# First attention: key sums by column quarters, and sums by feature computed with the head's sums as the stationary operand

## The reference

```python
logits = jnp.einsum('bhld,hdf->bhlf', k, W0) - 0.5 * jnp.sum(k * k, axis=-1, keepdims=True)
alpha = jax.nn.softmax(logits.reshape(B, H, L * NF), axis=2).reshape(B, H, L, NF)
N = jnp.einsum('bhlf,bhld->bhfd', alpha, v)      # key sums
D = jnp.sum(alpha, axis=2)
phi = jax.nn.softmax(jnp.einsum('bhld,hdf->bhlf', q, W0), axis=-1)
num = jnp.einsum('bhlf,bhfd->bhld', phi, N)
den = jnp.einsum('bhlf,bhf->bhl', phi, D)
out = num / (den[..., None] + EPS)
```

## Time and profile before

| | |
|---|---|
| median of three runs | 936.79 us |
| profiled execution, its own time | 937.28 us |
| its span, first to last instruction | 934.3 us |
| TensorE busy | 897.4 us, 96% |
| weight loads | 668.3 us, 72% |
| VectorE busy | 628.6 us, 67% |
| ScalarE busy | 307.8 us, 34% |
| GpSimd busy | 316.2 us, 34% |
| mean granted TensorE clock | 0.996 |

### The profile page before, as it was taken

The page is one execution under the profiler, slowest core; times in us unless marked ns, Lnnn a source line. Parts: engine busy times, 40 slices in busy tenths (PEclk is TensorE's granted clock), DMA queues, the critical chain, the costliest instruction groups (busy, mean ns, idle before and its releaser), DMA issues.

```text
span 934.3 us, 15873 instructions
## 1 busy us (share of the span) xinstructions
PE 897.4 (96%) x6316; PEld 668.3 (72%) x6316; DVE 628.6 (67%) x940; ACT 307.8 (33%) x494; POOL 316.2 (34%) x309
## 2 busy tenths in 40 slices
PE   6989999999999999999999998999999999999998
PEld 3668778877745444889976785888776445449998
DVE  4767566467554657978868574765774555778887
ACT  3645555210154445201133355641002443450000
POOL 5212412222375778356610023210005544771000
PEclk9999999999999999999999999999999999999999
DMA  8104000433143643366530000012222010216562
GB/s 272 38 22 136 1 1 1 142 99 112 60 136 88 210 135 76 104 176 187 159 118 1 2 1 1 2 53 90 67 81 79 1 26 2 68 37 179 177 198 91
DMA packets 46719, 80.07 MB, mean 86 GB/s; under 512 B 13047, under 2 KB 24023, under 8 KB 46647
## 3 DMA queue, kind: packets, MB, share of 16 engines
q1 hardware_dynamic: 46647, 79.07, 27.9%
HBM read 59.55 MB, written 19.33 MB: 84 GB/s over the span
## 4 chain that ended last, share of the span: by engine, by line
PE 83%; DVE 8%; issue 3%; ACT 2%; DMA 2%; POOL 1%; SPq 0%; POOLq 0%; DVEq 0%; ACTq 0%
PE ps L1213 19%; PE ps L1587 10%; PE ps L1492 6%; PE ps L1520 5%; PE ps L1432 5%; PE ps L1593 5%; PE ps L1386 5%; PE ps L1221 5%; PE ps L1338 3%; PE ps L1456 3%; PE ps L1400 3%; PE ps L1353 3%; DVE region L1057 2%; PE ps L1255 2%; PE ps L1292 2%
## 5 line engine op out<-in xcount | busy, mean ns | idle before, releaser
L611 POOL TENSOR_TENSOR xT<-xT,region 128x1024 f32<-128x1024 f32 (+5 forms) x80 | 127.7, 1596 | 92.2 <-PE ps L1520 63.8
L1132 DVE COPY_PREDICATED region<-region,ps 128x512 f32<-128x512 uint32 x112 | 82.5, 736 | 66.5 <-PE ps L1213 65.9
L1587 PE MATMUL ps<-expert_hi,k_hi 128*128 128x256 f32 x512 | 126.1, 284 | 0.7 <-DVE k_hi L1116 0.6
L1587 PE MATMUL ps<-expert_lo,k_hi 128*128 128x256 f32 x512 | 124.7, 281 | 0.0
L1057 DVE TENSOR_REDUCE region<-ps 128x2 f32<-128x1024 f32 (+2 forms) x96 | 89.0, 956 | 46.6 <-PE ps L1466 27.7
L1213 PE MATMUL ps<-expert_hi,wide_hi 128*128 128x512 f32 x256 | 102.3, 400 | 0.0
L1213 PE MATMUL ps<-expert_hi,wide_lo 128*128 128x512 f32 x256 | 99.9, 390 | 0.0
L1213 PE MATMUL ps<-expert_lo,wide_hi 128*128 128x512 f32 x256 | 99.8, 390 | 0.0
L1587 PEld LDWEIGHTS ps<-expert_hi,k_hi 128*128 128x128 f32 x512 | 97.3, 190 | 3.4 <-issue 3.4
L1587 PEld LDWEIGHTS ps<-expert_lo,k_hi 128*128 128x128 f32 x512 | 97.4, 190 | 0.0
L1116 DVE TENSOR_TENSOR k_hi<-region 128x1024 fp32r<-128x1024 f32 x64 | 80.7, 1262 | 19.9 <-PE ps L1593 19.7
(11 more groups left out here) (157 smaller groups left out, 1718.9 us busy)
## 6 DMA issues: line engine op xcount, KB each, us to landing
region<-hot_rows SPq DMA_DIRECT2D x128, 128.0 KB, 3.3
expert_hi<-halves_kept SPq DMA_DIRECT2D x22, 384.0 KB, 3.5
expert_lo<-halves_kept SPq DMA_DIRECT2D x22, 384.0 KB, 4.2
halves_kept<-expert_hi SPq DMA_DIRECT2D x16, 512.0 KB, 5.4
halves_kept<-expert_lo SPq DMA_DIRECT2D x16, 512.0 KB, 6.2
expert<-in_value_experts SPq DMA_DIRECT2D x8, 512.0 KB, 4.5
expert<-in_output_experts SPq DMA_DIRECT2D x8, 512.0 KB, 4.5
gb<-scale_rows SPq DMA_DIRECT2D x16, 256.0 KB, 3.9
```

The source lines that it names most:

```text
L611: pool.tensor_tensor(acc(c)[:, heads, lo:CH], acc(c)[:, heads, lo:CH], PT[:, k % RING, heads, lo:CH], ALU.add).then_inc(sem["added"], 1)
L1132: dve.copy_predicated(V3[:, t].rearrange("p (h k) -> p h k", k=HD3), chosen.unsqueeze(2).broadcast_to([P, H3, HD3]), ps[:, n % 4, :].rearr ...
L1587: mm(ps[:, 4 + t // 2, t % 2 * D:(t % 2 + 1) * D], k_hi[n % 2][:, t * P:(t + 1) * P], w[:, slot, columns], start=(n == 0 and t % 2 == 0 an ...
```

## The change

The key sums use four 32-column quarters of the array: one head at a time, 32 stationary columns (17 of them its own), 64 moving columns, 128 products for 64. N1w becomes 8 blocks of 32 columns, one copy instead of six, with no clearing; one epsilon product and one addition instead of three.

num is computed the other way round: `sums_turned(t)` takes a head's sums as the stationary operand (64 rows by 32 columns) and the turned features (64 rows by 128 columns) as the moving one, 16 products into banks 4 and 5. ScalarE copies the result (numT, 128x512), and 4 transposes bring it into bank 6. `sums_turned` stands right behind f in a step.

The first attention's maxima and subtractions are one instruction each of 1024 elements. In both attentions the product with Wo (now bank 7) and its VectorE work come ahead of num and its quotient, the norm's transposes use bank 5, and ScalarE copies the turned rows (`norm_evac`) ahead of the next `norm_apply`.

```diff
-    HALF = P // 2
+    HALF, QUARTER = P // 2, P // 4
 
     H1, HD1, NF = 16, 16, 64
     V1W = HD1 + 1
     PAIRS1 = H1 // 2
-    WIN = 3 * 2 * V1W
+
+    PAIR_AT = [4 * (k // 2 % 2) + 2 * (k // 4) + k % 2 for k in range(PAIRS1)]
...
-        V1_all = view((TT - 1) * H1 * V1W + (PAIRS1 - 1) * 2 * V1W + WIN)
+        V1_all = view(TT * H1 * V1W + HALF - 2 * V1W)
...
-        N1w = view(PAIRS1 * WIN).rearrange("p (k w) -> p k w", k=PAIRS1)
+        N1w = view(H1 * QUARTER // 2).rearrange("p (k w) -> p k w", k=PAIRS1)
+        N1_dens = N1w[:, :, HD1]
         at[0] = 0
-        N1T = view(CH)
+        N1T = view(2 * P)
+        numT = view(CH)
...
-        N1_RUNS = [(0, 1, 0), (1, PAIRS1 - 1, 2 * V1W), (PAIRS1 - 1, PAIRS1, 4 * V1W)]
...
-            return 7 if a else 3 if b else 4 + t % 2
+            return 5 if a else 3 if b else 4 + t % 2
...
-                until(pool, "oT_ready", b, 0)
-                pool.memset(N1w, 0.0).then_inc(sem["windows_clear"], 1)
-                until(pool, "windows_clear", b, 1)
...
-                        copy(N1T, ps[:, 4, :], "n_sb")
+                        copy(N1T, ps[:, 4, 0:2 * P], "n_sb")
+                    if 0 <= (t := s - 2) < TT:
+                        until(act, "numT_ps", b, t + 1)
+                        if t:
+                            until(act, "num_ps", b, t)
+                        copy(numT.rearrange("p (i s) -> p i s", i=2), ps[:, 4:6, 0:2 * P], "numT_sb")
...
+                    for a, t in due(s, 6):
+                        norm_evac(b, a + 1, t)
                     for a, t in due(s, 5):
                         norm_apply(b, a + 1, t)
                     for a, t in due(s, 6):
-                        norm_evac(b, a + 1, t)
...
                 def place_sums():
 
                     until(dve, "nT_ps", b, 1)
-                    until(dve, "windows_clear", b, 1)
-                    nT = ps[:, 5, :].rearrange("p (k w) -> p k w", w=HALF)
-                    for k0, k1, w0 in N1_RUNS:
-                        dve.tensor_copy(N1w[0:HALF, k0:k1, w0:w0 + V1W], nT[0:HALF, k0:k1, 0:V1W]
-                                        ).then_inc(sem["n_blk"], 1)
-                        dve.tensor_copy(N1w[HALF:P, k0:k1, w0 + V1W:w0 + 2 * V1W], nT[HALF:P, k0:k1, V1W:2 * V1W]
-                                        ).then_inc(sem["n_blk"], 1)
+                    dve.tensor_copy(N1w.rearrange("p k w -> p (k w)"), ps[:, 5, 0:2 * P]).then_inc(sem["n_blk"], 1)
 
...
+                        if a == 0:
+                            f = ps[:, 2:4, :].rearrange("p g (h f) -> p (g h) f", f=F)
+                            o = phi[:, i, 0:H * F].rearrange("p (h f) -> p h f", f=F)
+                            m = top[:, i, 0:H]
+                            dve.tensor_reduce(m, f, AX.X, ALU.max).then_inc(sem["top_ready"], DA)
+                            if s == 2:
+                                place_sums()
+                            if t >= 2:
+                                until(dve, "fT_ps", b, t - 1)
+                            until(dve, "top_ready", b, (t + 1) * DA)
+                            dve.tensor_tensor(o, f, m.unsqueeze(2).broadcast_to([P, H, F]), ALU.subtract
+                                              ).then_inc(sem["f_sub"], 1)
+                            continue
...
                         until(dve, "za_ps", b, 1)
-                        for k0, k1, w0 in N1_RUNS:
-                            dens = N1w[:, k0:k1, w0 + HD1:w0 + 2 * V1W:V1W]
-                            dve.tensor_tensor(dens, dens, ps[:, 6, 2 * k0:2 * k1].rearrange("p (a i) -> p a i", i=2),
-                                              ALU.add).then_inc(sem["n_ready"], 1)
+                        dve.tensor_tensor(N1_dens, N1_dens, ps[:, 6, 0:PAIRS1], ALU.add
+                                          ).then_inc(sem["n_ready"], 1)
+                    for a, t in due(s, 4):
+
+                        until(dve, "y_ps", b, a * TT + t + 1)
+                        until(dve, "bias_added", b, a * TT + t + 1)
+                        step(dve.tensor_tensor(X[:, b, t, :], ps[:, 7, 0:D], X[:, b, t, :], ALU.add))
+                        norm_stats(b, a + 1, t)
...
+                        until(dve, "num_ps", b, a * TT + t + 1)
+                        if a == 0:
+                            pairs = ps[:, 6, :].rearrange("p (i k w) -> p k i w", i=2, w=QUARTER)
+                            scale = rc[:, i, 0:H].rearrange("p (k i) -> p k i", i=2)
+                            step(dve.reciprocal(scale, pairs[:, :, :, HD]))
+                            if t >= 2:
+                                until(dve, "cxT_ps", b, t - 1)
+                            dve.tensor_tensor(cx[:, i, :].rearrange("p (k i w) -> p k i w", i=2, w=HD),
+                                              pairs[:, :, :, 0:HD],
+                                              scale.unsqueeze(3).broadcast_to([P, PAIRS1, 2, HD]),
+                                              ALU.mult).then_inc(sem["cx_ready"], 1)
+                            continue
                         num = ps[:, 6, 0:H * W].rearrange("p (h w) -> p h w", w=W)
...
-                    for a, t in due(s, 4):
-
-                        until(dve, "y_ps", b, a * TT + t + 1)
-                        until(dve, "bias_added", b, a * TT + t + 1)
-                        step(dve.tensor_tensor(X[:, b, t, :], ps[:, 5, 0:D], X[:, b, t, :], ALU.add))
-                        norm_stats(b, a + 1, t)
...
+                def sums_turned(t):
+
+                    until(pe, "fT_sb", b, t + 1)
+                    if t == 0:
+                        until(pe, "n_ready", b, 1)
+                    else:
+                        until(pe, "numT_sb", b, t)
+                        until(pe, "cxT_sb", b, t - 1)
+                        until(pe, "xT_ready", b, TT + max(0, t - 4))
+                    for k in range(PAIRS1):
+                        g, quarter = k // TC, slice(k % TC * QUARTER, (k % TC + 1) * QUARTER)
+                        for i in range(2):
+                            r = slice(i * HALF, (i + 1) * HALF)
+                            last = mm(ps[quarter, 4 + i, g * P:(g + 1) * P], N1w[r, k, :],
+                                      phT[r, t % 2, PAIR_AT[k] * P:(PAIR_AT[k] + 1) * P], start=True, stop=True)
+                    last.then_inc(sem["numT_ps"], 1)
+
...
+                    if 3 <= s < TT + 2:
+                        sums_turned(s - 2)
                     if s == 2:
                         until(pe, "n_sb", b, 1)
-                        for u in range(PAIRS1 // 2):
+                        for u in range(2):
                             last = pe.transpose(ps[:, 5, u * P:(u + 1) * P], N1T[:, u * P:(u + 1) * P], ident)
                         last.then_inc(sem["nT_ps"], 1)
                     for a, t in due(s, 1):
@@ -1354,37 +1390,45 @@
                                                 phi[:, t % 2, k * P:k * P + r], ident)
                         last.then_inc(sem["fT_ps"], 1)
                     if s == 2:
-                        until(pe, "n_blk", b, 2 * len(N1_RUNS))
-                        for k0, k1, w0 in N1_RUNS:
-                            last = mm(ps[:, 6, 2 * k0:2 * k1], eps_blk,
-                                      N1w[:, k0:k1, w0 + HD1:w0 + 2 * V1W:V1W], start=True, stop=True)
-                        last.then_inc(sem["za_ps"], 1)
+                        until(pe, "n_blk", b, 1)
+                        mm(ps[:, 6, 0:PAIRS1], eps_blk, N1_dens, start=True, stop=True).then_inc(sem["za_ps"], 1)
                     if s < 2:
 
                         until(pe, "e_ready", b, TT)
                         until(pe, "wv_ready", b, s + 1)
-                        for u in range(s * PAIRS1 // 4, (s + 1) * PAIRS1 // 4):
+                        for i in range(2):
                             for t in range(TT):
-                                for v in range(2):
-                                    c0, p = (t * PAIRS1 + 2 * u + v) * 2 * V1W, 2 * u + v
-                                    last = mm(ps[v * HALF:(v + 1) * HALF, 4, u * P:(u + 1) * P],
-                                              V1_all[:, c0:c0 + HALF], E1[:, t, p * P:(p + 1) * P],
+                                for q in range(TC):
+                                    h = 2 * (TC * s + q) + i
+                                    c0, f0 = (t * H1 + h) * V1W, (2 * s + i) * NF
+                                    last = mm(ps[q * QUARTER:(q + 1) * QUARTER, 4, f0:f0 + NF],
+                                              V1_all[:, c0:c0 + QUARTER], E1[:, t, h * NF:(h + 1) * NF],
                                               start=(t == 0), stop=(t == TT - 1))
                         last.then_inc(sem["n_ps"], 1)
+                    if s == 2:
+                        sums_turned(0)
+                    for a, t in due(s, 4):
+                        until(pe, "cxT_sb", b, a * TT + t + 1)
+                        if a + t:
```

(35 more changed lines are left out.)

10 lines of the change are left out of this document (3 added, 7 removed).

## The result

| | before | after |
|---|---|---|
| median of four runs | 937.08 us | 927.04 us |
| ratio, 95% interval | | 0.9896 [0.9882, 0.9911] |
| profiled execution, its own time | 937.28 us | 927.16 us |
| its span | 934.3 us | 925.4 us |
| mean granted TensorE clock | 0.996 | 1.000 |

What follows compares the result with a forecast made beforehand. TensorE was taken to bound most steps, until VectorE ends the shortened ones. Gains 5.0 + 9.7 + 0.4 less 2.5 for the clock, 12.6 off 937.28, gave 924.7, 924.2 at the median, rounded up to 924.5 us; range 920.5 to 928.

Steps and rivals of the forecast that it cites:

- The price of the quarters: Key sums: four column quarters run side by side, a 64-column round takes 0.056 us, 1.8 us per step instead of 3.5.
- two abreast: Rival on TensorE's tiles: only two served together, turned sums 1.85 us, key sums stay 3.5, about 943 us; chance 0.07.
- unhidden weight loads: Rival on the quarters: weight loads aren't hidden, 0.027 us more a round, 929 us; chance 0.07.
- Step 2: Chain over all engines after the key sums: six copies become one, 1.0 us less; f(3) 3.2 earlier in batch 0.
- the expert piece in batch 0: Head of step 3: ScalarE waits for the second piece, rounded at 72.2 us; of 3.2 us won 1.1 is left.
- the full step: Steady step with norm transposes: TensorE 4.39 us, VectorE 4.4, so 4.4 us for 5.16, 0.75 less.
- The step from f(4): Step without norm transposes, after the fifth f: said to take 4.15 us.
- The first rival: Steps come down only to 4.9 us, TensorE waiting at the numT transposes for ScalarE; 931 with a second clock fall; chance 0.18.
- part 7: Batch 0 after f(5): steps of 4.15, 4.4, 4.4 us, shorter step 8, the 512-row projection 5.0 us earlier.
- part 8: Batch 1: 4.0 us at f(3), 0.3, 0.7 to 0.9 for four steps, 1.2 for the last two, 1.4 clock: 9.7.
- part 9: Moved Wo product and norm_evac: same instructions, TensorE bound; earlier statistics save 0.2 us per batch, 0 at the low end.
- the third rival: Slower case: two abreast, 8.5 us lost over 16 steps, 2 saved by VectorE's copies, about 943 us; chance 0.07.

Runs made afterwards that it cites:

- key_serial: Changed kernel, but the key sums take one column quarter after the other instead of going round the four; 941.73 us in a single execution.
- drain_banks: Changed kernel, but the norm's transposes of tiles 1 and 2 after the first attention go to banks 2 and 3, not bank 5; 926.91 us.
- drain_order: Changed kernel with those norm transposes in bank 2, late cx transposes in bank 3, and ScalarE's numT copy ahead of turned rows and norm in steps 7 to 9; 924.58 us.
- copy_late: Changed kernel, but ScalarE does the next norm's rows ahead of its copy of the turned rows, as before the change; 932.51 us.
- first_product_late: Changed kernel, but in the first attention the Wo product goes behind num, its VectorE work behind the quotient, as before the change; 928.56 us.
- cross_both: Changed kernel, but in the cross attention TensorE's product with W2o and VectorE's sum and statistics go back behind num and its quotient; 926.89 us.
- key_halves: Changed kernel with the earlier key sums on two 64-column halves, so the output is not the reference's; 932.71 us.
- all_three_filled: Kernel of drain_order plus cross_both with batch 0's second expert piece rounded later (920.6 us), plus 12 unread TensorE transposes per batch; 920.9 us.

## Why the forecast held, and which of its steps didn't

**Right.** The wins are read from the windows; only the key sums' quarters and the two moves were undone in runs, the turned sums, the merged maxima and the shorter step 2 were not. The price of the quarters: 0.056 us for a round of four. 1.93 us for a step of key sums (1.8), 0.60 for the turned sums (0.55), 0.44 for the transposes. The two rivals that spoke against the quarters are out: two abreast would have given 1.85 us for the turned sums, and unhidden weight loads, at the 0.027 us of the prediction, would have made 2.8 us of a step's key sums (32 rounds of 0.083 and a change of division). The loads of the key sums share all rows and take 0.110 us each in the profile, while `key_serial`, on one quarter at a time, starts a record every 0.052 us, so they lie beside other records. The rule of the Trainium skill (TensorE: Matmul & The Clock Gate, "Part 3: Packing small matmuls — row/col tiling") that a weight load overlaps matmuls in flight only where the row group differs isn't borne out by this; the same section also lets a load run ahead into a background weight buffer, which these times would fit. Step 2 (6.15 us) and batch 1 up to f(3) (-3.92 for -4.0) came as worked out, and undoing the key sums cost 1.65 and 2.5 us in the same stretches. So did the expert piece in batch 0: ScalarE waits for it, starts it at 72.08 us (forecast 72.2), and TensorE waits behind it for numT.

```profile
72.08 1.06 ACT L631 ACTIVATE expert_hi<-expert 128x1024 fp32r<-128x1024 f32 x1 [1.52 <-DMA expert<-in_value_experts]
73.68 0.66 PE L1423 MATMUL ps<-const,region 128*128 128x128 f32 x4 [1.58 <-ACT region L631]
```

The cut of the full step is 0.50 us (0.61 in batch 1), that of the step after it 0.57, for 0.75 and 0.66.

**The steps from f(4) and f(6): too low, for a wait that wasn't in the sum.** The full step was said to be 4.4; measured are 4.66, 4.55 and, up to the end of its last transposes, 4.49. The step from f(4) was said to be 4.15 and takes 4.67 and 4.61. In the latter the profile names the wait, between f and the turned sums (batch 1):

```profile
527.31 0.36 ACT L631 ACTIVATE region<-ps 128x256 f32<-128x256 f32 x1
527.93 0.67 PE L1354 MATMUL ps<-region 64*32 64x128 f32 x32 [0.34 <-ACT region L631]
```

The sums need bank 4, and ScalarE reads cx out of it behind the exponential. The first weight load of the sums starts at 527.90 us, 0.23 after that copy's end. In the step from f(6) it starts 0.22 us after the end of the same copy in both batches, 1.19 and 1.18 us after f where the step from f(7) has 1.07: a wait of some 0.1 us of the same kind, too short for a bracket. (In batch 0 the sums of that step also take 0.71 us for 0.60; why is open.) VectorE begins its maxima 1.25 us after f's start in the steps from f(6) and f(7) alike, so it doesn't hold them. The first rival had the mechanism, ScalarE in order late behind the exponential, but at the numT transposes and for 0.5 us in every full step; no row of a full step shows that.

**Steps 8 and 9: the step of the forecast that failed** (part 7, "f(7) 3.4 earlier. Step 8 loses 1.76 of num and gains 1.1, and waits for the last exponential", and the 1.2 us of part 8). Neither step became shorter; 1.6 and 1.9 us of forecast gain were not there. I had counted TensorE's work and forgotten what f's 1.06 us hide in a full step: the turned sums write banks 4 and 5, which ScalarE has to read first, in its own order, behind the exponential. Without an f ahead of them the sums wait for it. `drain_banks` showed that it isn't the one bank. With both banks free and ScalarE's order changed (`drain_order`) the steps have their forecast length, and 1.8 us a batch come back; `copy_late` shows that the order alone, with the banks shared, moves them by 1.8 us the other way. How the gain of `drain_order` divides between second bank and order is not shown. The waits were in the diff, as lines of `sums_turned`.

**The moved product** was put at nothing or a little gain (part 9). In the first attention it is worth 0.65 us a batch by `first_product_late`, by covering the copy of numT; in the cross attention it costs 0.5, since it uncovers the copy of cx in the last steps. `cross_both` takes that back.

**Key sums of batch 0.** f(2) came 1.17 us earlier and not 2.1. Of the missing 0.9, 0.77 is the late end of the key sums, marked "issue": f(1) to f(2) takes 4.79 us in batch 0 and 4.02 in batch 1. It is there, ahead of the same last four records, in all ten other kernels whose quarters are interleaved (4.78 to 5.33 us in batch 0) and in neither `key_halves` nor `key_serial` (5.73 and 8.77, as in batch 1). That the instructions come too slowly is one reading; it wasn't tested, and the cause is open.

**The clock.** I had taken two falls to 1.2 GHz, 2.5 us, as the price of more idle time. The profiled execution has none before its last microseconds. More than that: the 19 executions of the kernel before in the first session all have a mean clock of 0.995 to 0.998, most of them 0.996, which is its profile's two falls (in batch 1 behind step 2, and at 402.71 us); the changed kernel has 1.000 in three of four. So of the 8.9 us of its span some 3 (1.4 and 1.5) are falls that are gone, the work in the touched stages gives 7.4 (2.75 + 5.6 - 1.0), and 1.4 go back, nearly all in the third attention. There VectorE waits 1.25 us (batch 0) and 1.26 us (batch 1) for the transfer gb<-scale_rows and waited 0.45 and 0.57 before; whether the edit or the single execution makes that isn't shown. The forecast had 13.7 us of work and -1.1 of clock. That it came so near is luck: two errors of opposite sign met. The drain and the end of the cross attention were too hopeful by 5.0 us together (1.7, 2.0 and 1.4) and the other stretches by 1.3, the clock was too gloomy by 4.0. (Part 8's 9.7 us add up only with the low end of its 0.7 to 0.9 a step; the third rival's sum is 943.8.) (In the profiled execution's own time the gain is 10.1 us, 1.2 more than in its span: around the span of the earlier trace rows lie 3.0 us, around this one 1.8, as in most executions of either kernel.)

A fall behind step 2 does exist in kernels with the change: four of the first eight experiments have one there in one of the batches, and `copy_late` too. What decides it is open. Step 2 takes 6.15 to 6.17 us in nearly all of them, with a fall behind it or without, and `all_three_filled` neither confirms nor excludes it, as its partner had no fall to remove.

## What to carry to other kernels

When work is taken off the bounding engine in a pipeline by hand, check its last steps by themselves: there the products that covered the copies of the steady state are missing, and a bank that a new product shares can become a wait. When a product moves in one engine's list, move its readers in the other lists with it; here half the move back cost 4.4 us a batch, the whole one won 0.5. And read each execution's granted clock before crediting an edit: here a third of the gain in the span came from falls of the clock that the edit did not aim at.

## What the hardware showed beyond that

Four 32-column quarters of 128 rows run abreast: a round of four records of 64 columns takes 0.056 us, while records of one quarter alone follow each other every 0.052 us, with weight loads that take 0.110 us each. Eight tiles of 64 rows by 32 columns with 128 moving columns run abreast too (32 records between starts of 0.60 us, the change of division in it). In the second step of key sums of batch 0 the last four of 128 such short records come 0.48 to 1.03 us late in all eleven kernels with interleaved quarters; the same products in batch 1 run through. No run shows why.
